# Shorter opening run of maxima, setup steps moved into the main loop, and the two PV steps of a round set apart

## The chip, the cores and the metric
The kernel runs on one core of one Trainium2 chip. Time is device time of one execution in microseconds (us). Before the change the median of three runs is 1162.82 us (1160.92 to 1167.73). The engines are PE (TensorE: matmuls and transposes), DVE (VectorE), ACT (ScalarE), POOL (GpSimd) and SP, which here only issues DMAs. Each runs its own list of instructions strictly in order and waits on semaphores.

## The reference
One transformer block with adaptive layer norm, float32, on x of 4 batches x 1024 tokens x 256 features:

```
mod = silu(c) @ wmod  -> sa, ca, ga, sb, cb, gb   (ga, gb: pushed to at least 0.25 in size)
h = layernorm(x) * (1 + ca) + sa
x = x + ga * (softmax(q k^T / 4) v @ proj_w.T + proj_b)     16 heads of 16
h = layernorm(x) * (1 + cb) + sb
per group of 1024 tokens: of 8 encoders/decoders take the one with the least
  mean((relu(h We + be) Wd + bd - h)^2); its adapter is relu(h Wdown + bd) Wup + bu
x = x + gb * (h W_base + b_base + adapter)
```

## The kernel before
Attention of the four batches is the main loop. It is cut into 256 units: a unit is 4 heads, one half of the queries (512) and 128 keys. For each unit PE does four "E" matmuls (keys x queries, transposed scores, 50 rows: 48 of split operands and two rows that hold minus the row maximum), ACT takes the exponential of each into `P` (L831), and PE does the unit's "PV" step (`PV`, four groups of 17 columns in the single bank `pO`). The row maxima that the two extra rows hold come from "M" matmuls (queries x keys, `pM`), which DVE reduces one by one (L953). 32 M belong to the 8 units of one head group and query half ("hq", 0 to 31). After the 32nd, `mmax` joins them on DVE, POOL splits them in two halves (L1255), PE transposes them (`mturn`, L605), ACT copies them (L846), and SP writes them into the operand `QO` with four DMAs (L1358). M must therefore run ahead of E. E uses three banks (`pE`), M three banks (`pM`), everything else mostly one bank (`pX`).

All engines walk one list of steps, made by `order()` on the host. It has three parts. First the opening: layer norm, q, k and v of batch 0. Then `LEAD` (56) M steps with nothing of E between them; there M takes five banks in turn (`pM` and two of `pE`). Between each five of them stands one item of `beside`: `setupa`, `setupb`, `setupq`, `setupc` (products of decoder weights and biases that later choose the adapter, with DVE work behind each) and two halves of `qk 0,1,0` (the next query projection). Then 128 rounds of the main loop. I call them **pair 0 to pair 127**, since each has two units: 8 E, up to 8 M, two PV. A pair is three bursts of 3, 3 and 2 E/M couples (`BURSTS`). Behind burst 1 stand PV of the two units before. Behind bursts 2 and 3 stand "long" steps (pieces of projection, encoder, gram and so on) in number set by a credit, taken from the table of due units in `plan()`; "short" steps (transposes) stand behind burst 3, "quiet" steps (no PE) in between. A pair that finds no long step due has only E, M and PV for PE. Batch b begins at pair 32b.

A query or key projection (`qk`) leaves PSUM as `hi` (ACT, L881) and `lo` (DVE, L1048), and SP then copies pieces of both into `QO` or `KO` with twelve DMAs (`copy`, L1349). There is one `hi`/`lo` buffer: the next `qk` can write `hi` only when all twelve have landed. The copies stand in SP's list two per burst, and so do `mturn`'s four DMAs, in the order of the list; SP waits at `mturn` until ACT has written `mT`.

Of the kernel before, what the change touches and what calls it, by code (L numbers as in the profile page):

```python
# [11 lines left out]
ALU = mybir.AluOpType  # L12
# [9 lines left out]
NM = 32 * 8 * NB  # L22
# [14 lines left out]

SHARE = 1.45

LEAD = 56  # L40

MB, EB, XB, SB = (0, 1, 2), (3, 4, 5), (6,), (5, 2)

SEQ = [(gi, c) for gi in range(4 * NB - 4) for c in range(2)]
# [4 lines left out]
def plan():  # L51

    due = {}

    def at(u, *steps):
        due.setdefault(u, []).extend(steps)

    at(0, ("gates",))
    at(5, ("qk", 0, 1, 1, 0), ("qk", 0, 1, 1, 1))
    for b in range(NB + 1):  # L60
        B = UB * b
        if b >= 1:
            q = b - 1
            halves = ((B - 31, (0, 1)), (B, (2, 3))) if q == LAST else ((B + 3, (0, 1, 2, 3)),)
            for u, ks in halves:
                for th in sorted({k // 2 for k in ks}):
                    if q == LAST or th == 1:
                        at(u - 1, ("atturn", q, th), ("atturn", q, 2 + th))
                for k in ks:
                    at(u, ("proj", q, k), ("bn2", q, k), ("ln2s", q, k), ("ln2n", q, k), ("xsq", q, k))  # L70
                    at(u, ("xturn", q, k))
                for t in range(2 * ks[0], 2 * ks[-1] + 2):
                    at(u + 1, ("enc", q, t))
                for p in range(4):
                    at(u + 2, ("half", q, p, ks[0] // 2) if q == LAST else ("gram", q, p))
            at(B + 6, ("pick", q), ("select", q), ("fetch", q))
            if q == LAST:
                for k in range(4):
                    at(B + 6 if k > 1 else B - 10, ("base", q, k))
            for h in range(2):  # L80
                at(B + 7, ("mid", q, h), ("out", q, 2 * h), ("out", q, 2 * h + 1))
        if b < NB:
            if b:
                at(B + 0, ("qk", b, 1, 0, 0), ("qk", b, 1, 0, 1))
                at(B + (4 if b == LAST else 6), ("qk", b, 1, 1, 0), ("qk", b, 1, 1, 1))
            if b < LAST:
                at(B + 55, ("atturn", b, 0), ("atturn", b, 2))
            at(B + (36 if b == LAST else 60), ("prep", b))
        if b + 1 < NB:
            for k in range(4):  # L90
                at(B + 11, ("ln1load", b + 1, k), ("ln1s", b + 1, k), ("ln1n", b + 1, k), ("ln1turn", b + 1, k))
            at(B + 33, ("qk", b + 1, 0, 0, 0), ("qk", b + 1, 0, 0, 1))
            at(B + 38, ("qk", b + 1, 0, 1, 0), ("qk", b + 1, 0, 1, 1))
            at(B + 44 if b else B + 18, *(("v", b + 1, k) for k in range(4)))
    return due


def before(s):

    if len(s) == 1:  # L100
        return []
    kind, b, a = s[0], s[1], s[2:]
    if kind == "ln1load":
        return [(("ln1turn", b, a[0] - 1), 0)] if a[0] else []
    if kind == "ln1s":
        return [(("ln1load", b, a[0]), 1)]
    if kind == "ln1n":
        return [(("ln1s", b, a[0]), 1)]
    if kind == "ln1turn":
        return [(("ln1n", b, a[0]), 1)] + ([(("qk", b - 1, 1, 1, 1), 0)] if b else [])  # L110
    if kind == "qk":
        return [(("ln1turn", b, 2 * a[2] + i), 1) for i in range(2)]
    if kind == "v":
        return [(("ln1turn", b, a[0]), 1)]
    if kind == "atturn":

        return [(("oturn", turned(b, a[0])), 1)] + ([(("gram", b - 1, 3), 0)] if b else [])
    if kind == "prep":
        return [(("out", b - 1, 3), 1)] if b else []
    if kind == "proj":  # L120
        return [(("atturn", b, a[0] // 2 + i), 0) for i in (0, 2)] + [(("prep", b), 4)]
    if kind == "bn2":
        return [(("proj", b, a[0]), 0)]
    if kind == "ln2s":
        return [(("bn2", b, a[0]), 0)]
    if kind == "ln2n":
        return [(("ln2s", b, a[0]), 1)]
    if kind == "xsq":
        return [(("ln2n", b, a[0]), 1)]
    if kind == "xturn":  # L130
        return [(("ln2n", b, 2 * (a[0] // 2) + i), 1) for i in range(2)]
    if kind == "enc":
        return [(("xturn", b, 2 * (a[0] // 4) + i), 1) for i in range(2)]
    if kind == "gram":
        return [(("enc", b, t), 1) for t in range(8)]
    if kind == "half":
        return [(("enc", b, 4 * a[1] + t), 1) for t in range(4)]
    if kind == "base":
        return [(("xturn", b, 2 * (a[0] // 2) + i), 1) for i in range(2)]
    if kind == "pick":  # L140
        return [(("half", b, 3, 1) if b == LAST else ("gram", b, 3), 0)] + [(("xsq", b, k), 0) for k in range(4)]
    if kind == "select":
        return [(("pick", b), 1)]
    if kind == "fetch":
        return [(("select", b), 0)]
    if kind == "mid":
        return [(("fetch", b), 2)]
    if kind == "out":
        return [(("mid", b, a[0] // 2), 0)] + ([(("base", b, a[0]), 0)] if b == LAST else [])
    return []  # L150
# [7 lines left out]
def copies(n, w):  # L158


    return [("copy", n, w, g, i) for g in (0, 1) for i in range(12 if (n, w, g) == (0, 0, 0) else 6)]


def order():
# [4 lines left out]
    for w in (1, 0):  # L169
        for half in range(2):  # L170
# [3 lines left out]

    out += [(("v", 0, t), p) for t in range(4) for p in range(2)] + [("modmm", 1), ("modmm", 2)]

    beside = deque([[("setupa",)], [(("qk", 0, 1, 0, 0), p) for p in range(2)], [("setupb",)],
                    [(("qk", 0, 1, 0, 1), p) for p in range(2)], [("setupq",)], [("setupc",)]])
    for i in range(LEAD):
        out.append(("M", i))  # L180
        if i % 5 == 4 and beside:
            out += beside.popleft()
        if i == 31:
            out.append(("mmax", 0))
        if i == 37:
            out.append(("mturn", 0))
    due, m = plan(), LEAD
    moving, waiting, begun = deque(copies(1, 0)), {"short": [], "long": [], "quiet": []}, []
    done = {("ln1turn", 0, k): -9 for k in range(4)}

    def come(u):
# [5 lines left out]
    def next_of(queue, u):  # L197

        if queue == "long" and begun:
            return begun.pop()  # L200
        for s in waiting[queue]:
            if all(done.get(p, u + 1) + lag <= u for p, lag in before(s)):
                waiting[queue].remove(s)
                return (s, 0) if s[0] in PIECES else s
        return None

    def put(s, u):
        out.append(s)
# [33 lines left out]
    for u0 in range(0, NU, 2):  # L242
        if u0 % 8 == 0 and u0:
            waiting["short"].append(("oturn", u0 // 8 - 1))
        come(u0)
        come(u0 + 1)
        tiles = deque((u0 + i // 4, i % 4) for i in range(8))
        for n, pairs in enumerate(BURSTS):
            u = u0 + 2 * n / 3
            if n == 2:  # L250

                short = [s for s in (next_of("short", u) for _ in range(2)) if s]
            for _ in range(pairs):
                out.append(("E", *tiles.popleft()))
                maximum()
            for _ in range(3 if u0 >= UB * LAST else 2):
                if moving:
                    out.append(moving.popleft())
            s = next_of("quiet", u)
            if s:  # L260
                put(s, u)
            if n == 0:
                if u0:
                    out += [("PV", u0 - 2), ("PV", u0 - 1)]
            else:
                if n == 2:
                    for s in short:
                        put(s, u)
                credit = long(u, min(credit + (SHARE if u0 < UB * LAST else 2), 2.5))
            s = next_of("quiet", u)  # L270
            if s:
                put(s, u)
# [84 lines left out]
def adaln_block(nc, x, wqkvT, wpT, pb, wbase, bbase, wenc, benc, bencc, wdec, wdecT, bdecT,  # L357
                wdown, bdown, wup, bup, cidx, cT, wmod, consts, out):
    ctx = ExitStack()
    with ctx:  # L360
# [577 lines left out]
        def vector(e):  # L938
# [4 lines left out]
            for s in S.list:  # L943
# [58 lines left out]
                elif kind == "gates":  # L1002
# [3 lines left out]
                    for k, o in ((0, 512), (1, 1280)):  # L1006
# [8 lines left out]
                                               in1=gt[:, k, 1, :], op0=ALU.add,  # L1015
                                               op1=ALU.mult).then_inc(*(link.up() if k == 0 else (s_gates, 1)))

                elif kind == "ln1s":
                    b, k = s[1:]
                    xt = tokens(b, k)  # L1020
# [151 lines left out]
                                    ALU.add).then_inc(*empties(s))  # L1172

                elif kind == "setupa":
                    e.memset(be[:, :, :], 0.0).then_inc(*link.up())
                    dve.wait_ge(*link.now())
                    dve.wait_ge(d_w[2], 16)
                    dve.wait_ge(d_cst, 16)
                    for p in range(4):
                        a = e.tensor_scalar(be[:, p, 2 * p:2 * p + 2], bmask, bec[:, p:p + 1], None, ALU.mult)  # L1180
                    a.then_inc(s_be, 1)
                    dve.wait_ge(*full(*s))
                    dve.wait_ge(d_w[3], 16)
                    e.tensor_tensor(bT[:, :, :], bank(s)[:, 0:16].rearrange("p (c n) -> p c n", c=2), bdT[:, :, :],
# [262 lines left out]
```

## Time and profile before

| | |
|---|---|
| median of three runs | 1162.82 us |
| the profiled execution | 1166.85 us |
| its span | 1165.0 us |
| PE busy | 1085.9 us (93%), 5820 matmuls |
| DVE busy | 814.1 us (70%) |
| ACT busy | 643.3 us (55%) |
| M reductions, DVE L953 | 630.0 us in 1002 recorded (1024 in the program) |
| mean granted TensorE clock | 0.94 of 2.4 GHz |

The span runs from the first to the last instruction of the profiled execution, which lies 1.85 us under its own time and 4.0 us over the median with it. PE's busy share reads higher than its work: E and M matmuls that follow each other at the pace of DVE are recorded as overlapping. The places of pairs in time are read from the starts of the 1024 E matmuls, all of which are in the trace: pair 0 starts at 85.03 us, pair 7 at 140.28, pair 15 at 200.98, pair 32 at 324.85, pair 112 at 969.86 and pair 127 at 1097.99.

### The profile page before, as it was taken

To read this page: it belongs to the slowest core of one execution; us is meant where nothing else is said; L and a number is where in the kernel's file an instruction comes from. 1 tells how busy PE (TensorE), PEld (TensorE's weight loads), DVE (VectorE), ACT (ScalarE), POOL (GpSimd) and SP (SyncE) were. 2 spreads that over 40 slices of the span, in tenths; PEclk is the share of its full clock that TensorE was granted. 3 is DMA by queue.
4 is the path that set the end of the run, shared out by engine and by line. 5 is a ranking of instruction groups with operands and counts; after the bars stand their busy time and mean duration, and the time that the engine had idled before them with its cause. 6 is when DMAs were issued, how large, how long until landed. Compare 5 with 4: busy or idle time off the path is not lost.

```text
span 1165.0 us, 15950 instructions
## 1 busy us (share of the span) xinstructions
PE 1085.9 (93%) x5820; PEld 512.3 (44%) x5820; DVE 814.1 (70%) x1593; ACT 643.3 (55%) x1293; POOL 126.4 (11%) x251
## 2 busy tenths in 40 slices
PE   6898999989999999999999999999999999989966
PEld 3443344333334345454444344455443455434534
DVE  3486777767878887786778887777688766672133
ACT  3105667656756666665666666665666555556510
POOL 3000121000030121000301120000300000210000
PEclk9757899988999999999999999999899999979989
DMA  7612400240115100330233000411170000200001
GB/s 224 95 19 38 65 20 10 39 58 15 41 40 76 28 19 2 56 60 29 64 55 64 11 20 10 73 34 38 55 100 11 2 2 14 83 1 2 1 1 41
DMA packets 31345, 47.02 MB, mean 40 GB/s; under 512 B 6611, under 2 KB 23512, under 8 KB 31260
## 3 DMA queue, kind: packets, MB, share of 16 engines
q1 hardware_dynamic: 30564, 45.15, 19.6%
q0 software_dynamic: 288, 0.79, 0.4%
q8 instruction: 46, 0.75, 0.3%
q14 instruction: 31, 0.25, 0.1%
q10 hardware_dynamic: 416, 0.07, 0.0%
HBM read 15.95 MB, written 4.22 MB: 17 GB/s over the span
## 4 chain that ended last, share of the span: by engine, by line
PE 72%; DVE 11%; ACT 6%; SPq 3%; DMA 3%; issue 2%; POOL 1%; ACTq 0%; DVEq 0%; POOLq 0%
PE pX L558 21%; PE pO L558 21%; PE pE L558 18%; PE pM L558 10%; DVE mx L953 6%; ACT P L831 4%; DMA QO<-lo 2%; SPq L1349 2%; ACT hi L881 1%; DVE lo L1048 1%; SPq L1347 1%; DMA x<-in_x 1%; SPq L1358 1%; PE pE L635 1%; DVE X L1084 1%
## 5 line engine op out<-in xcount | busy, mean ns | idle before, releaser
L953 DVE TENSOR_REDUCE mx<-pM 128x1 f32<-128x512 f32 x1002 | 630.0, 683 | 178.4 <-PE pM L558 176.5
L831 ACT ACTIVATE P<-pE 128x512 f32<-128x512 f32 x1024 | 544.5, 599 | 334.5 <-PE pE L558 333.1
L558 PE MATMUL pE<-QO,KO 50*128 50x512 f32 x1024 | 373.4, 452 | 18.8 <-ACT P L831 12.8
L558 PE MATMUL pM<-KO,QO 48*128 48x512 f32 x1002 | 373.8, 469 | 12.0 <-DVE mx L953 9.2
L558 PEld LDWEIGHTS pE<-QO,KO 50*128 50x128 f32 x1024 | 170.1, 191 | 273.9 <-issue 194.4
L558 PE MATMUL pO<-P,V 128*17 128x512 f32 x2048 | 268.6, 646 | 0.0
L558 PEld LDWEIGHTS pM<-KO,QO 48*128 48x128 f32 x1002 | 165.5, 193 | 46.8 <-DVE mx L953 35.5
L558 PEld LDWEIGHTS pO<-P,V 128*17 128x17 f32 x2048 | 49.3, 101 | 140.5 <-issue 140.2
L558 PE MATMUL pX<-h1T,wqkv_s 128*128 128x512 f32 x116 | 65.6, 676 | 9.1 <-DVE lo L1048 8.2
L1255 POOL CAST mh<-mxc 128x16 fp32r<-128x16 f32 x32 | 6.5, 204 | 544.6 <-DVE mxc L962 544.6
L558 PE MATMUL pX<-wenc_s,h2T 128*128 128x512 f32 x108 | 55.0, 619 | 1.5 <-DVE Hb L1103 1.2
L558 PE MATMUL pX<-X,Hb 128*128 128x258 f32 x200 | 51.5, 393 | 1.2 <-DVE lo L1048 1.1
L558 PEld LDWEIGHTS pX<-X,Hb 128*128 128x128 f32 x200 | 35.4, 190 | 13.3 <-issue 7.3
L881 ACT ACTIVATE hi<-pX 128x512 fp32r<-128x512 f32 x28 | 16.7, 598 | 42.6 <-PE pX L558 22.8
L838 ACT ACTIVATE osb<-pO 128x512 f32<-128x512 f32 x32 | 19.1, 598 | 37.7 <-PE pO L558 37.7
L1048 DVE SCALAR_TENSOR_TENSOR lo<-pX,hi 128x512 fp32r<-128x512 f32 x28 | 19.4, 691 | 27.4 <-ACT hi L881 27.4
L558 PEld LDWEIGHTS pX<-h1T,wqkv_s 128*128 128x128 f32 x116 | 20.3, 203 | 32.1 <-issue 18.8
L1103 DVE TENSOR_TENSOR Hb<-pX,nbe 128x512 f32<-128x512 f32 x27 | 18.5, 686 | 18.2 <-PE pX L558 18.2
L558 PE MATMUL pX<-Hb 128*128 128x128 f32 x216 | 30.6, 292 | 0.0
L558 PEld LDWEIGHTS pX<-Hb 128*128 128x128 f32 x216 | 28.1, 202 | 5.0 <-issue 4.5
L558 PE MATMUL pX<-wbg,h2T 128*128 128x256 f32 x112 | 29.6, 389 | 0.2 <-ACT mid L936 0.2
L1240 POOL TENSOR_SCALAR xin<-xin,mv,rs 128x256 f32<-128x256 f32 x24 | 29.3, 1227 | 1.1
(211 smaller groups left out, 764.9 us busy)
## 6 DMA issues: line engine op xcount, KB each, us to landing
QO<-hi SPq DMA_DIRECT2D x60, 128.0 KB, 4.4
KO<-hi SPq DMA_DIRECT2D x56, 128.0 KB, 4.1
x<-in_x SPq DMA_DIRECT2D x4, 1024.0 KB, 7.1
out<-x SPq DMA_DIRECT2D x16, 256.0 KB, 2.2
QO<-lo SPq DMA_DIRECT2D x30, 128.0 KB, 4.6
KO<-lo SPq DMA_DIRECT2D x28, 128.0 KB, 4.5
xin<-in_x SPq DMA_DIRECT2D x12, 256.0 KB, 2.7
QO<-mT SPq DMA_DIRECT2D x128, 4.0 KB
```

The source lines that it names most:

```text
L558: return e.matmul(o, lhsT, rhs, start=start, stop=stop)
L635: a = e.transpose(o[:, 256 * c + 128 * t:256 * c + 128 * t + 128], tokens(b, k)[:, t, 128 * c:128 * c + 128], ident)
L831: e.activation(P[:, u % 3, j, :], bank(s), ACT.Exp).then_inc(*empties(s))
L838: e.activation(osb[:, :], pO[:, :], ACT.Copy).then_inc(s_osb, 1)
L881: e.activation(halves(oc, w, b)[0][:, cs], bank(s), ACT.Copy, scale=1.0 if w else 0.25).then_inc(s_hi, 1)
L953: e.tensor_reduce(mx[:, hq % 2, k:k + 1, kh], bank(s), AX.X, ALU.max, negate=True).then_inc(*empties(s))
L1048: e.scalar_tensor_tensor(out=lo_[:, cs], in0=bank(s), scalar=1.0 if w else 0.25, in1=hi_[:, cs].bitcast(F), op0=ALU.mult, op1=ALU.subtract ...
L1084: e.scalar_tensor_tensor(out=X[:, t, 0:D], in0=x2[:, t, :], scalar=mv2[:, t, 0:1], in1=bc[:, 2, :], op0=ALU.subtract, op1=ALU.mult).then_i ...
L1103: e.tensor_tensor(Hb[:, t, :], bank(s), nbe[:, :], ALU.max).then_inc(*empties(s))
L1240: a = e.tensor_scalar(xt[:, t, :], xt[:, t, :], mv1[:, k, t, 0:1], rs1[:, k, 1, t:t + 1], ALU.subtract, ALU.mult)
L1347: e.dma_start(*move(0, 0, 0, i, src, slice(512 * c, 512 * c + 512))).then_inc(d_q0[c], 16)
L1349: e.dma_start(*move(w, slot, g, i, src)).then_inc(landed(n, w, g)[0], 16)
```

## The change
`LEAD` goes from 56 to 48. `beside` is gone: its `qk` halves become due in unit 0, the four setup steps in unit 8 with an order among them (`SETUP`), and `gates` in unit 4. DVE's filling of `be` moves from `setupa` into `gates`. The copies of `qk 0,1,0` now enter SP's list when that step is done. And the second PV of a pair moves from behind burst 1 to behind burst 2 wherever fewer than two long steps are ready and M steps are left; there the credit is cut so that at most one long step follows.

```diff
-LEAD = 56
+LEAD = 48
+SETUP = {"setupb": [(("setupa",), 1)], "setupq": [(("setupb",), 1)], "setupc": [(("setupq",), 0)]}
...
-    at(0, ("gates",))
-    at(5, ("qk", 0, 1, 1, 0), ("qk", 0, 1, 1, 1))
+    at(0, ("qk", 0, 1, 0, 0), ("qk", 0, 1, 0, 1))
+    at(6, ("qk", 0, 1, 1, 0), ("qk", 0, 1, 1, 1))
+    at(4, ("gates",))
+    at(8, ("setupa",), ("setupb",), ("setupq",), ("setupc",))
...
-    beside = deque([[("setupa",)], [(("qk", 0, 1, 0, 0), p) for p in range(2)], [("setupb",)],
-                    [(("qk", 0, 1, 0, 1), p) for p in range(2)], [("setupq",)], [("setupc",)]])
     for i in range(LEAD):
         out.append(("M", i))
-        if i % 5 == 4 and beside:
-            out += beside.popleft()
...
-    moving, waiting, begun = deque(copies(1, 0)), {"short": [], "long": [], "quiet": []}, []
+    moving, waiting, begun = deque(), {"short": [], "long": [], "quiet": []}, []
...
+    def ready(u):
+
+        return len(begun) + sum(all(done.get(p, u + 1) + lag <= u for p, lag in before(s)) for s in waiting["long"])
...
             if n == 0:
                 if u0:
-                    out += [("PV", u0 - 2), ("PV", u0 - 1)]
+                    out.append(("PV", u0 - 2))
+
+                    later = m < NM and ready(u) < 2
+                    if not later:
+                        out.append(("PV", u0 - 1))
             else:
                 if n == 2:
                     for s in short:
                         put(s, u)
+                elif u0 and later:
+                    out.append(("PV", u0 - 1))
+                    credit = min(credit, 1 - SHARE)
                 credit = long(u, min(credit + (SHARE if u0 < UB * LAST else 2), 2.5))
```

PE, behind the first ten M steps or so, before (M is written to pM and pE from KO,QO; `be,wd` and `bT,Hb` are setupa and setupb, `h1T,wqkv_s` is qk 0,1,0):

```order
L558 MATMUL pE<-be,wd 128x8 x8
L558 MATMUL pM<-KO,QO 128x512 x3
L558 MATMUL pE<-KO,QO 128x512 x2
L558 MATMUL pX<-h1T,wqkv_s 128x512 x2
L558 MATMUL pM<-KO,QO 128x512 x3
L558 MATMUL pE<-KO,QO 128x512 x2
L558 MATMUL pE<-bT,Hb 128x8 x8
```

PE at the end of the opening run, after; the last row is the first E of pair 0 (operands QO,KO):

```order
L570 MATMUL pM<-KO,QO 128x512 x3
L617 MATMUL pE<-cst,mhl 32x128
L570 MATMUL pE<-KO,QO 128x512 x2
L570 MATMUL pM<-KO,QO 128x512 x3
L570 MATMUL pE<-KO,QO 128x512 x2
L570 MATMUL pM<-KO,QO 128x512 x3
L570 MATMUL pE<-QO,KO 128x512
```

The opening run now has M alone, apart from the transpose of hq 0's maxima (`mhl`), and ends eight M earlier.

SP from the DMAs of hq 0's maxima (`QO<-mT`) to those of hq 1's, before (`QO<-hi`, `QO<-lo` are the copies of qk 0,1,0, `modd<-X` belongs to gates):

```order
L1358 DMA QO<-mT 2x4x128 x4
L1349 DMA QO<-hi 16x2x1024 x2
L1349 DMA QO<-lo 16x2x1024
L1349 DMA QO<-hi 16x2x1024
L1363 DMA modd<-X 4x1536
L1349 DMA QO<-hi 16x2x1024
L1349 DMA QO<-lo 16x2x1024
L1349 DMA QO<-hi 16x2x1024 x2
L1349 DMA QO<-lo 16x2x1024
L1349 DMA QO<-hi 16x2x1024 x2
L1349 DMA QO<-lo 16x2x1024
L1358 DMA QO<-mT 2x4x128 x4
```

The same copies on SP after:

```order
L1371 DMA QO<-mT 2x4x128 x4
L1362 DMA QO<-hi 16x2x1024 x2
L1362 DMA QO<-lo 16x2x1024
L1362 DMA QO<-hi 16x2x1024
L1376 DMA modd<-X 4x1536
L1362 DMA QO<-hi 16x2x1024
L1362 DMA QO<-lo 16x2x1024
L1371 DMA QO<-mT 2x4x128 x4
L1362 DMA QO<-hi 16x2x1024 x2
L1362 DMA QO<-lo 16x2x1024
L1362 DMA QO<-hi 16x2x1024 x2
L1362 DMA QO<-lo 16x2x1024
```

Six of the twelve copies now stand behind hq 1's maxima. In batch 1 and 2's query copies (pairs 17 to 19, 33 to 35, 65 to 67) four stand behind the maxima, where before ten stood behind them but a pair earlier.

PE in pair 23, which has no long step, after, from its first PV (unit 44) to its second (45); `free` and a number is the bank that is waited for (`order` rows with their waits):

```order
L570 MATMUL pO<-P,V 17x512 x4
L570 MATMUL pE<-QO,KO 128x512 [waits free3]
L570 MATMUL pM<-KO,QO 128x512 [waits free0]
L570 MATMUL pE<-QO,KO 128x512 [waits free4]
L570 MATMUL pM<-KO,QO 128x512 [waits free1]
L570 MATMUL pE<-QO,KO 128x512 [waits free5]
L570 MATMUL pM<-KO,QO 128x512 [waits free2]
L570 MATMUL pO<-P,V 17x512 x4
```

And before, pair 23 from its first burst to both PV:

```order
L558 MATMUL pE<-QO,KO 128x512 [waits free3]
L558 MATMUL pM<-KO,QO 128x512 [waits free0]
L558 MATMUL pE<-QO,KO 128x512 [waits free4]
L558 MATMUL pM<-KO,QO 128x512 [waits free1]
L558 MATMUL pE<-QO,KO 128x512 [waits free5]
L558 MATMUL pM<-KO,QO 128x512 [waits free2]
L558 MATMUL pO<-P,V 17x512 x8
```

One row of eight PV matmuls has become two of four with three E/M couples between them. This holds in 48 of the 128 pairs.

## Rows read from the trace of the kernel before
**Rows 1.** Windows: stretch, its us; busy us of each engine; granted clock, DMA share.
```profile
37.20:85.03 47.83, 40.97 (x118) 22.67 (x118) 37.55 (x78) 2.05 (x4) 0.57 (x3) 0.62 0.32 48
85.03:140.28 55.25, 49.08 (x223) 19.78 (x223) 40.64 (x76) 31.73 (x61) 4.55 (x10) 0.80 0.34 54
140.28:200.98 60.70, 57.35 (x315) 26.25 (x315) 44.69 (x84) 40.55 (x81) 11.30 (x18) 0.94 0.05 15
200.98:324.85 123.87, 114.41 (x588) 44.14 (x589) 89.76 (x153) 78.14 (x151) 7.46 (x18) 0.92 0.21 39
206.80:215.78 8.98, 8.74 (x42) 3.31 (x42) 6.56 (x11) 5.87 (x11) 0.00 (x0) 1.00 0.00 0
228.81:241.46 12.65, 10.37 (x38) 3.20 (x39) 6.75 (x11) 5.38 (x10) 0.00 (x0) 0.81 0.65 84
248.38:257.06 8.68, 7.76 (x34) 2.70 (x33) 6.01 (x13) 4.34 (x9) 0.58 (x3) 0.80 0.82 122
277.42:283.95 6.53, 5.94 (x34) 2.49 (x34) 5.37 (x12) 4.06 (x9) 0.57 (x3) 1.00 0.02 4
350.93:360.57 9.64, 8.56 (x39) 3.09 (x39) 8.28 (x18) 5.79 (x13) 0.94 (x2) 1.00 0.57 71
603.53:613.55 10.02, 8.57 (x40) 3.09 (x39) 8.27 (x18) 5.79 (x13) 0.93 (x2) 1.00 0.62 76
969.86:1097.99 128.13, 122.06 (x637) 58.50 (x636) 65.07 (x139) 71.56 (x144) 13.78 (x26) 0.92 0.07 23
1097.99:1165.04 67.05, 45.91 (x211) 28.25 (x210) 20.05 (x62) 10.48 (x25) 3.31 (x6) 0.90 0.06 18
```
**Rows 2.** Waits of DVE, 37 to 85 us: total, times, longest.
```profile
DVE lo L1048 <- ACT hi L881: 4.7, 2, 3.5
DVE bT L1184 <- PE pE L558: 3.3, 1, 3.3
```
**Rows 3.** Timeline of DVE in the opening run: start, us, instruction.
```profile
39.72 1.28 DVE L953 TENSOR_REDUCE mx<-pE 128x1 f32<-128x512 f32 x2
...
76.52 1.88 DVE L953 TENSOR_REDUCE mx<-pM 128x1 f32<-128x512 f32 x3
...
79.51 1.88 DVE L953 TENSOR_REDUCE mx<-pM 128x1 f32<-128x512 f32 x3
```
**Rows 4.** Timeline of PE: setupa and setupc in the opening run.
```profile
41.79 3.17 PE L558 MATMUL pE<-be,wd 128*128 128x8 f32 x16 [3.08 <-issue]
...
65.72 3.78 PE L558 MATMUL pX<-Hb 128*128 128x128 f32 x16
```
**Rows 5.** Timeline of DVE in pair 25, with its idle time before.
```profile
281.87 3.08 DVE L953 TENSOR_REDUCE mx<-pM 128x1 f32<-128x512 f32 x5 [1.10 <-PE pM L558]
```
**Rows 6.** Waits of DVE, 140 to 229 us.
```profile
DVE mx L953 <- PE pM L558: 20.4, 15, 2.5
```
**Rows 7.** Waits of DVE, 241 to 325 us.
```profile
DVE mx L953 <- PE pM L558: 21.9, 15, 2.9
```
**Rows 8.** Pairs 19, 35: SP's timeline, the chain of waits, ACT's timeline.
```profile
223.75 2.62 SPq L1358 DMA_DIRECT2D QO<-mT  x4
...
232.12 6.23 DMA QO<-lo
...
238.43 0.60 ACT L881 ACTIVATE hi<-pX 128x512 fp32r<-128x512 f32 x1 [2.35 <-DMA QO<-lo]
...
358.14 0.60 ACT L881 ACTIVATE hi<-pX 128x512 fp32r<-128x512 f32 x1 [0.82 <-PE pX L558]
```
**Rows 9.** Timeline of PE behind the last E.
```profile
1107.49 0.63 PE L669 MATMUL pM<-cst,Atok 128*128 128x128 f32 x4 [0.97 <-DVE Atok L978]
1108.89 1.97 PE L558 MATMUL pX<-wpg,h1T 128*128 128x256 f32 x8 [0.78 <-ACT h1T L903]
...
1133.01 1.98 PE L558 MATMUL pE<-X,Hb 128*128 128x258 f32 x8 [0.88 <-DVE Hb L1103]
...
1135.71 1.91 PE L558 MATMUL pE<-X,Hb 128*128 128x258 f32 x8
```

More of the change, by code:

```diff
@@ L100, in before @@
     if len(s) == 1:
-        return []
+        return SETUP.get(s[0], [])
     kind, b, a = s[0], s[1], s[2:]
@@ L1016, in vector @@
                                                op1=ALU.mult).then_inc(*(link.up() if k == 0 else (s_gates, 1)))
+                    e.memset(be[:, :, :], 0.0).then_inc(*link.up())
+                    dve.wait_ge(*link.now())
+                    dve.wait_ge(d_w[2], 16)
+                    dve.wait_ge(d_cst, 16)
+                    for p in range(4):
+                        a = e.tensor_scalar(be[:, p, 2 * p:2 * p + 2], bmask, bec[:, p:p + 1], None, ALU.mult)
+                    a.then_inc(s_be, 1)
                 elif kind == "ln1s":
@@ L1174, in vector @@
                 elif kind == "setupa":
[L1175 to L1181, printed above, removed]
                     dve.wait_ge(*full(*s))
```

## The prediction, made before the changed kernel was timed
> **What bounds the kernel now.** I read the page first: PE is busy 93% of the span and DVE 70%, so most of the loop is PE's, but that share hides who sets the pace. Then the table of windows, cut at the starts of pairs. Where pairs carry long steps, PE has real work throughout: pair 16, with three qk pieces, takes 8.98 us with PE busy 8.74 [rows 1]. Pairs with none take far more than their PE work: pair 25 takes 6.53 us at full clock. Its eight reductions come every 0.60 us (five in 3.08), and before them DVE stood idle for 1.10 us, waiting for PE [rows 1, 5]. So such a pair is 8 x 0.60 = 4.8 us of reductions, some 0.3 of other DVE work, and a hole in which PE did 16 PV matmuls in a row while the three M banks ran empty. The holes add up to 20.4 us in pairs 7 to 18 and 21.9 us in pairs 20 to 31 [rows 6, 7].
>
> The opening run, 37.20 to 85.03 us, is DVE's as well: five reductions start in 79.51 - 76.52 = 2.99 us, 0.598 each [rows 3], while the clock is mostly at its lower level, 1.2 GHz (mean 0.62) [rows 1]. DVE also waits there for steps that stand between M: 4.7 us for `hi`, 3.3 for setupa [rows 2]. The end, from pair 112, is a chain of dependent steps beside the last E [rows 1].
>
> **The opening run.** M 0 to 4 are reduced by 39.72 + 1.28 = 41.0 us [rows 3]. With nothing between, DVE goes straight on. Pair 0's first E takes the bank that M 43 leaves: 39 further reductions x 0.598 = 23.3 us and one mmax, so 64.5 us, where it started at 85.03. Could something else hold it? It needs hq 0's maxima in `QO`. M 31 is reduced at 41.0 + 27 x 0.598 = 57.1; the way from there through POOL, PE, ACT and four DMAs I estimate at 6 us (2.62 for the four issues [rows 8], the rest small instructions and a landing): 63, just in time. **-20** (-18 to -21).
>
> **Pairs 0 to 6** hold 55.25 us [rows 1]. Added: four qk pieces at (8.98 - 6.53) / 3 = 0.8 us each [rows 1], 3.3 us. The setup steps: setupa and setupc took 3.17 and 3.78 us at 1.2 GHz [rows 4], so half at 2.4; with setupb about 5 us on PE, and 3 us on DVE beside it. Bounds: 0, if all falls into holes of pairs 4 to 6, and 9 at the lower clock; I take 4. Gained: qk fills PE in pairs 0 and 1, so I expect the clock back earlier than now, where the stretch has a mean of 0.80 [rows 1]: -4.
>
> Then the wait that the change adds. `hi` of qk 0,1,1 (pair 3) is free when twelve copies have landed. Six of them now stand on SP behind the four DMAs of hq 1's maxima, and SP waits at those until ACT has run at the end of pair 2. Queued behind is everything of SP; who waits is ACT at `hi`, with its exponentials behind it, hence PE's E banks. From the start T of pair 3: ACT and the first issue 0.8 us, the four DMAs 2.62, five issues of 0.63 to the last, and 6.23 from that issue to landing [rows 8]: T + 12.8. Pair 19 is the measured example: its last copy landed at 232.12 + 6.23 = 238.35, that is T + 9.5, ACT waited 2.35 us, and the pair took 12.65 [rows 1, 8], 3.1 more than the landing. So pair 3 should take 15.9 where some 8.5 were enough: +7. Bounds: 0, if copies overlap better than in pair 19, and +9 with the lower clock behind it. `gates` on DVE gets `be` with it: 0.7 us more in pair 2, covered by three filled M banks only in part; +0.3. Sum: 3.3 + 4 - 4 + 7.3 = 10.6; since four of these pairs also get the split PV I take **+8** (-3 to +14).
>
> **Pairs 7 to 14** hold 60.70 us [rows 1], all eight with PV split. Between two bursts PE is now away for one PV instead of two, so of the 1.10 us hole [rows 5] I expect some 0.2 to remain: -0.9 at full clock, up to twice that at half clock. With v pieces the second half of the gain is PE's own, since five couples no longer follow each other at DVE's pace. The 20.4 us of holes [rows 6] lie over 12 pairs, 1.7 each; I take 1.0 of it: **-8** (-12 to 0).
>
> **Pairs 15 to 31** hold 123.87 us [rows 1]; all but pairs 16 and 19 split. 21.9 us of holes in twelve pairs are 1.8 each [rows 7]; 15 pairs x 0.95 = 14. Against it pair 19: four copies stand behind hq 5's maxima, which come a pair later, so the last lands at T + 0.8 + 2.62 + 3 x 0.63 + 6.23 = T + 11.5 instead of 9.5: +2. **-12** (-20 to +2).
>
> **Pairs 32 to 111** are PE's; pieces move between pairs, their sum stays. Pair 35 had no such wait (0.82 us, for PE [rows 8]) and took 9.64 us; with landing at T + 11.5 and 3 us behind it, 14.2. Pair 67 took 10.02 [rows 1] and goes the same way. That is +4.4 each. In pair 98 the maxima move behind all copies, -1.5, and the four near-empty pairs at the ends of batches 1 and 2 give -2. **+5** (0 to +12).
>
> **The end.** Split pairs may place one long step only, so out 2 ends a pair later, prep 3 and proj 3 with it; xturn 3 moves from pair 120 to 122 and 123, and eight `half` and four `base` pieces that stood in pairs 124 to 126 now stand in and behind pair 127. From 969.86 to 1097.99 are 128.13 us [rows 1]. Without the twelve pieces (three half pieces take 1135.71 - 1133.01 = 2.7 us [rows 9], so 11 us) they take at most 117. I take 116. Behind 1097.99, the waits of 0.97 and 0.78 us [rows 9] take in about 2 of the 11 us: 67.05 + 9 = 76. **-3** (-12 to +8).
>
> Also moved and priced at nothing: each hq's maxima come one pair later relative to their E. From transpose to last landing I estimate 5 to 6 us (2.62 of it the issues [rows 8]); a pair is left for it. If pairs drop under 5.5 us, E waits by the difference, eight hq's of a few tenths.
>
> **Sum.** -20 + 8 - 8 - 12 + 5 - 3 = -30 us, on the profiled execution's 1166.85 us: 1137. That execution lies 4.0 us over the median of the runs, so I predict 1162.8 - 30.5 = 1132 us. Differences under 0.5%, 6 us, can't be told from no change.
>
> **Rivals.**
> 1. The split gives nothing: the exponentials or bank turns take the place of the hole. For it: ACT's eight exponentials are 4.06 us of pair 25's 6.53 [rows 1], and they stall at each PV too. Against: they leave 2.4 us. Then -8 and -14 go: the sum is -8.5: 1154.
> 2. The deferred pieces are not absorbed: the end costs +12 instead of -3, because xturn 3 stands in pairs that are short of PE work and the rest of the chain starts later. For it: 67.05 us behind pair 127 with PE busy for 45.91 [rows 1]. Against: twelve pieces leave pairs that had been full. 1132 + 15 = 1147.
> 3. More comes out: copies land as in pair 19 at worst (7 + 2 + 9 us not lost) and holes close fully. 1132 - 18 = 1114.
> 4. Slower: the clock. The split spreads PE's work thin, and the opening run shows the clock at 0.62 where M alone runs at DVE's pace [rows 1]. Pair 21, without a long step and at a mean of 0.80, took 8.68 us [rows 1] against 6.8 for the 15 pairs on average ((123.87 - 8.98 - 12.65) / 15). If the 22 or so pairs without long steps all went that way, +1.9 x 22 = +42 would stand in place of -22. With the other terms, -8, that is +34: 1197. It decides from 8 / 22 = 0.36 us more per pair than today. Against it: today's runs of couples without a PV between are longer than any that are left, and the stretch 200.98 to 324.85 still holds a mean of 0.92 [rows 1].
>
> The Trainium skill (TensorE: Matmul & The Clock Gate, A second HAM failure mode: psum-queue depth-cycling) says that a PE which idles briefly and often between groups of matmuls, as it goes round PSUM banks, swings between its two clocks. This speaks for rival 4, since the change doubles the switches between E/M and PV; the trace has such swings in these pairs, but with PE's pauses as long as they are before the split.
>
> **Chances.** The forecast 52%, with its own range 1121 to 1143; rival 3 15%; rival 1 14%; rival 2 12%; rival 4 7%. Faster: all of the forecast and of 3, nearly all of 2 and two thirds of 1 (it ends 9 us below, with 6 the bound): 0.88. Within: the rest of 1 and 2, 0.06. Slower: 0.06. From 1115 to 1156 I leave out rival 4, half of rival 3 and the edge of 1: 2 in 10.
>
> **What would show it.** The first E matmul at 64 to 66 us. Eight reductions in a row every 0.6 us with no hole over 0.3 in pairs 20 to 31, and that stretch (241.46 to 324.85 now, 6.9 us a pair) at 5.5 to 6.2 us a pair. ACT waiting for DMA at `hi` in pairs 3, 19, 35 and 67, by 4 to 7 us in pair 3. The stretch behind pair 127 at 75 to 77 us. A first E after 68 us, low clock in most split pairs, or E waiting for `mT`'s DMAs would make the forecast wrong.

## The result, and the profile after
The changed kernel takes 1153.02 us (median of nine runs, 1148.24 to 1158.81), the kernel before 1162.82 us in the same comparison. The ratio is 0.990 (95% interval 0.987 to 0.993): 9.8 us faster, where 30.5 were forecast. A second comparison gave 1153.0 us against 1165.4, ratio 0.9895 (0.988 to 0.991).

The profiled execution took 1148.24 us. It is the fastest of its nine, 4.8 us below their median, while that of before lay 4.0 above its own. So the two profiles differ by 18.6 us, and 8.8 of that is the choice of executions. The totals say little:

```profile
span 1146.4 us, 15955 instructions
PE 1064.5 (93%) x5820; PEld 494.6 (43%) x5820; DVE 814.1 (71%) x1593; ACT 644.1 (56%) x1293; POOL 127.0 (11%) x251
PEclk8668899899999999999999999999999999988989
```

The windows, cut at the starts of pairs, do (columns as in [rows 1]: the stretch, its us, busy us of PE, PEld, DVE, ACT and POOL, granted clock, DMA share, GB/s). In order: the opening run, pairs 0 to 6, 7 to 14, 15 to 31, 35, 67, 112 to 126, and what is behind the start of pair 127.

```profile
37.20:62.87 25.67, 25.09 (x45) 11.55 (x44) 25.64 (x45) 0.27 (x1) 0.57 (x3) 0.54 0.41 63
62.87:131.64 68.77, 60.24 (x283) 25.58 (x282) 46.84 (x99) 33.30 (x63) 4.54 (x10) 0.77 0.32 51
131.64:185.44 53.80, 52.82 (x315) 22.70 (x314) 45.19 (x84) 39.93 (x79) 11.30 (x18) 0.97 0.06 16
185.44:294.94 109.50, 100.41 (x590) 37.25 (x589) 90.14 (x153) 77.82 (x152) 11.04 (x23) 0.95 0.24 45
...
318.75:330.08 11.33, 8.80 (x40) 3.13 (x39) 8.88 (x20) 5.80 (x14) 0.94 (x2) 0.98 0.29 49
574.58:585.74 11.16, 8.63 (x39) 3.13 (x38) 8.70 (x20) 5.79 (x14) 0.94 (x2) 0.99 0.29 50
944.33:1070.12 125.79, 113.16 (x598) 47.98 (x597) 67.44 (x139) 71.01 (x143) 14.02 (x26) 0.92 0.08 23
...
1070.12:1146.44 76.32, 57.37 (x271) 37.93 (x270) 22.92 (x76) 10.58 (x25) 3.31 (x6) 0.90 0.05 16
```

Against [rows 1]: the first E came at 62.87 us instead of 85.03. Pairs 7 to 31 took 163.3 us instead of 184.6, and their clock rose. Pairs 0 to 6 took 68.8 instead of 55.3. Pairs 112 to 126 took 125.8 where 116 were forecast, and 76.3 us follow, as forecast.

The holes of DVE have shrunk. These are its waits for PE in pairs 7 to 18 and 20 to 31 (131.64 to 211.72 and 224.30 to 294.94 us; total, times, longest), and the five reductions of pair 25 with the idle time before them; they answer to [rows 5 to 7].

```profile
DVE mx L965 <- PE pM L570: 10.1, 15, 1.6
```
```profile
DVE mx L965 <- PE pM L570: 7.7, 14, 1.7
```
```profile
259.38 3.16 DVE L965 TENSOR_REDUCE mx<-pM 128x1 f32<-128x512 f32 x5 [0.24 <-PE pM L570]
```

20.4 us have become 10.1, and 21.9 have become 7.7; the 1.10 us hole of pair 25 is 0.24.

The first of the two large waits of the changed kernel stands in pair 3 (87.14 to 104.67). SP's timeline, the chain of waits with the last copy's way to memory, and ACT's timeline; they answer to [rows 8].

```profile
90.65 2.62 SPq L1371 DMA_DIRECT2D QO<-mT  x4
93.31 1.23 SPq L1362 DMA_DIRECT2D QO<-hi  x2
...
96.48 0.59 SPq L1362 DMA_DIRECT2D QO<-lo  x1
```
```profile
96.48 4.73 DMA QO<-lo
```
```profile
101.29 0.60 ACT L893 ACTIVATE hi<-pX 128x512 fp32r<-128x512 f32 x1 [4.27 <-DMA QO<-lo]
```

Six copies follow `mT`'s four issues, and ACT sits 4.27 us before `hi`, with the exponentials behind it.

The second is in pair 118 (993.41 to 1006.03 us). POOL's timeline, and PE's with the transpose of hq 30's maxima:

```profile
996.22 1.30 POOL L1285 TENSOR_TENSOR wpg<-wp_s,bc 128x512 f32<-128x512 f32 x1 [35.55 <-DMA bc<-modd]
...
999.52 5.49 POOL L1296 TENSOR_TENSOR x<-x,bc 128x256 f32<-128x256 f32 x8
1004.94 0.20 POOL L1268 CAST mh<-mxc 128x16 fp32r<-128x16 f32 x1
...
1005.36 0.22 POOL L1274 TENSOR_TENSOR mhl<-mxc,mh 128x16 f32<-128x16 f32 x1
```
```profile
1005.73 0.37 PE L617 MATMUL pE<-cst,mhl 128*32 128x128 f32 x1 [7.37 <-POOL mhl L1274]
```

`prep 3` (8.8 us on POOL, from 996.22 to 1005.01) stands ahead of the splitting of the maxima, so PE idles for 7.37 us at `mturn 30`. It already stood there before the change, where PE came later and waited 1.93 us. These are the same rows of the kernel before:

```profile
1016.80 5.53 POOL L1283 TENSOR_TENSOR x<-x,bc 128x256 f32<-128x256 f32 x8 [0.70 <-DMA x<-in_x]
1022.27 0.20 POOL L1255 CAST mh<-mxc 128x16 fp32r<-128x16 f32 x1
```
```profile
1023.06 0.37 PE L605 MATMUL pE<-cst,mhl 128*32 128x128 f32 x1 [1.93 <-POOL mhl L1261]
```

From about the start of the wait of the changed kernel to the end of pair 119 the mean clock is 0.70, and pair 119 takes 9.3 us:

```profile
998.02:1015.36 17.34, 9.97 (x45) 3.73 (x41) 6.39 (x11) 5.59 (x11) 7.50 (x13) 0.70 0.01 3
```

Pairs 117 to 119 together took 26.87 us before and 27.25 now. Their mean clock is 0.81 in both. These are the rows of pairs 117 to 119 before, and of pairs 121 to 126 before and now:

```profile
1013.21:1040.08 26.87, 24.07 (x118) 10.72 (x117) 18.11 (x38) 13.28 (x27) 10.74 (x18) 0.81 0.08 26
1051.53:1097.99 46.46, 46.38 (x249) 23.01 (x250) 8.00 (x27) 27.52 (x55) 0.58 (x3) 1.00 0.00 1
```
```profile
1023.43:1070.12 46.69, 42.90 (x202) 15.96 (x201) 14.39 (x34) 28.79 (x62) 1.83 (x5) 0.93 0.00 1
```

By the lists of steps, pairs 121 to 126 held 24 pieces of long steps before and hold 12 now, with the last eight M in pair 121. They take as long as before.

### The profile page after: what moved, and what is told of

Same layout as the page of the kernel before. It is cut to its first block, busy times and chain, and to the rows that moved or that the text cites. A ratio compares the mean times of both kernels' runs of the same rounds, so it can differ in the third digit from the quotient of the medians.

```text
span 1146.4 us, 15955 instructions
## 1 busy us (share of the span) xinstructions
PE 1064.5 (93%) x5820; PEld 494.6 (43%) x5820; DVE 814.1 (71%) x1593; ACT 644.1 (56%) x1293; POOL 127.0 (11%) x251
## 4 chain that ended last, share of the span: by engine, by line
PE 77%; DVE 10%; ACT 4%; DMA 3%; SPq 3%; issue 2%; POOL 1%; ACTq 0%; DVEq 0%
PE pX L570 23%; PE pE L570 20%; PE pO L570 20%; PE pM L570 10%; DVE mx L965 5%; DMA QO<-lo 2%; ACT P L843 2%; SPq L1362 1%; DVE lo L1068 1%; ACT hi L893 1%; SPq L1371 1%; DVE X L1104 1%; PE pE L681 0%; PE pE L617 0%; POOL x L1296 0%
## 5 line engine op out<-in xcount | busy, mean ns | idle before, releaser
L570 PE MATMUL pE<-QO,KO 50*128 50x512 f32 x1024 | 367.4, 449 | 15.1 <-ACT P L843 7.3
L570 PEld LDWEIGHTS pO<-P,V 128*17 128x17 f32 x2048 | 43.0, 98 | 116.1 <-issue 116.1
L570 PE MATMUL pX<-X,Hb 128*128 128x258 f32 x208 | 54.5, 395 | 2.4 <-DVE lo L1068 1.5
L1123 DVE TENSOR_TENSOR Hb<-pX,nbe 128x512 f32<-128x512 f32 x26 | 17.9, 687 | 29.7 <-PE pX L570 29.7
L570 PE MATMUL pX<-wqkv_s,h1T 128*128 128x256 f32 x104 | 27.1, 391 | 0.9 <-DVE accA L1132 0.9
```

The costliest lines, as they stand in the source:

```text
L570: return e.matmul(o, lhsT, rhs, start=start, stop=stop)
L1123: e.tensor_tensor(Hb[:, t, :], bank(s), nbe[:, :], ALU.max).then_inc(*empties(s))
```

## The experiments
Each ran in five rounds beside the kernel before, whose median was 1165.4 us in the first four, 1164.0 in the next four and 1164.7 in the last four. "The change" stands for its second measurement, 1153.0 us. Theory A is the forecast's mechanism plus two waits that eat it: copies behind maxima on SP, and maxima behind `prep` on POOL. The rivals are told in each expectation. Stretches are read from one execution, which does not always lie at its kernel's median: the profiled ones of experiments 2 and 9 are 4.9 and 6.4 us under it, those of 3, 4, 6, 11 and 12 are 4.9, 3.2, 6.7, 3.2 and 3.7 us over it, and the others lie within 1.4 us.

**1. The change once more.**

> The changed kernel once more, unedited, for a second profile. The first one was of its fastest execution (1148.2 us against a median of 1153.0), the one of before lay 4 us over its median. Theory A (the two profiles tell the terms right, and what differs between executions of one kernel is the clock in a few pairs): pair 0 again at 62.9 us within 1 us, pair 3 at 16 to 18 us, pairs 20 to 31 within 3 us of the first profile, and the span differs by the granted clock in single pairs, 2 to 8 us in all. Rival B (the gain of the split pairs was luck of that one execution): pairs 20 to 31 take 5 us or more longer than in the first profile.

1153.0 us (1150.5 to 1155.4). Its profile is close to its median (1153.53 us). Two stretches, pairs 121 to 126 and what is behind the start of pair 127, show what one execution of this kernel has and another has not:

```profile
1022.05:1073.92 51.87, 48.69 (x203) 18.03 (x202) 14.37 (x34) 29.13 (x62) 1.83 (x5) 0.77 0.00 1
1073.92:1151.73 77.81, 58.94 (x271) 38.13 (x270) 22.92 (x75) 10.59 (x25) 3.31 (x6) 0.87 0.05 16
```

Pairs 121 to 126 at a mean clock of 0.77 are 51.87 x 0.23 / 0.5 = 24 us at 1.2 GHz. The first profile had 6.8 us of it there, and 46.7 us in all. Everything ahead of pair 118 repeats within 0.5 us.

**2. The split alone.** Before, with the split of PV and its cap; `ready` is the same as in the change. POOL's `fetch` also waits for its own earlier split of maxima, which stands ahead of it in POOL's own list.

```diff
-                    out += [("PV", u0 - 2), ("PV", u0 - 1)]
+                    out.append(("PV", u0 - 2))
+                    later = m < NM and ready(u) < 2
+                    if not later:
+                        out.append(("PV", u0 - 1))
...
+                elif u0 and later:
+                    out.append(("PV", u0 - 1))
+                    credit = min(credit, 1 - SHARE)
```

> The kernel before with the PV split and its limit on long steps alone; opening, LEAD 56 and copies as before. (A wait of POOL for its own last instruction is added before the fetch step.) Theory A (opening -22, first pairs +13, split -21 in pairs 7 to 31, copies behind the maxima +4 to +7, end +7, the end by the split's limit): pair 0 stays at 85 us, no wait for the copies in pairs 3 and 35, pairs 7 to 31 shorter by 15 to 20 us, the stretch from pair 112 on 3 to 8 us longer than before: 1145 to 1152 us. Rival B (the end's loss is of the eight M steps that come later, not of the split): the end is as before, 1140 to 1145. Rival C (the split gives little without the new opening): 1158 or more.

1147.6 us, ratio 0.984 (0.982 to 0.987): better than the whole change. Pairs 20 to 31 take 69.5 us instead of 83.4, pairs 0 to 6 52.7 instead of 55.3, and the stretch behind pair 127 takes 76.0: that 9 us is the split's, by its cap. But pairs 112 to 120 take 74.0 us instead of 81.7 and pairs 121 to 126 44.7 instead of 46.5, so from pair 112 to the end it is 194.7 us against 195.2 before, not the 3 to 8 us more that were expected.

**3. All but the split.**

```diff
-                    later = m < NM and ready(u) < 2
+                    later = False
```

> The changed kernel with the PV split taken out (both PV behind burst 1 everywhere); LEAD 48, moved setup steps and copies stay. Theory A: pair 0 at 63 us, pair 3 about 17 us, pair 7 at about 133 us (7 us earlier than before), pairs 7 to 31 as before, pairs 35 and 67 longer by 1.5 to 3 us each, the end within 3 us of before: 1155 to 1161 us. Rival B: the end 7 us longer than before also here, so 1163 or more.

1159.8 us, ratio 0.996 (0.994 to 0.998). The first E comes at 63.0 us, and most of these 22 us is lost again: pairs 0 to 6 take 70.1 us instead of 55.3, pairs 32 to 111 649.6 instead of 645.0, and pairs 20 to 31

```profile
232.63:319.50 86.87, 82.86 (x411) 32.15 (x410) 61.14 (x105) 54.11 (x105) 10.43 (x20) 0.85 0.19 38
```

against 70.64 with the split and 83.4 before. Behind pair 127 stand 66.9 us. The two parts alone give 17.8 + 5.6 = 23.4 us, together 12.4, which is 11 short. In the profiles this loss stands at the end: from pair 112 on, each part alone takes 194.7 and 193.7 us (before: 195.2), both together 206.9 (experiment 1).

**4. The change with LEAD 56** (and the wait at `fetch` as in 2). Everything else of the change is kept.

```diff
-LEAD = 48
+LEAD = 56
```

> The changed kernel with LEAD 56 again; setup steps stay in the main loop, split stays. (A wait of POOL for its own last instruction is added before the fetch step.) Theory A (most of the opening's gain is the steps taken from between M, not the eight M; hq's maxima come a pair earlier again and the copies stand before them less): pair 0 at 67.7 us (eight reductions of 0.6 later), pair 3 shorter than 17.5 us since the six copies no longer stand behind the maxima of hq 1, about 12 us, pairs 35 and 67 1 to 3 us shorter: 1146 to 1152 us, a few us under the changed kernel. Rival B (the eight M count in full, nothing comes back): 1157 us or more.

1141.9 us, ratio 0.978 (0.976 to 0.980): 11 us faster than with 48, although the first E comes 7.3 us later. The maxima now stand elsewhere against copies and `prep`: pairs 35 and 36 take 17.1 us (21.7), 67 to 69 24.9 (29.7), pair 3 14.6 (17.5), and 117 to 119 21.0 (25.4 to 27.3); in pairs 117 to 119 PE has no wait for POOL. The time lies under the range expected, 1146 to 1152. This turned "48 instead of 56" into the question.

**5. Copies ahead of the maxima, LEAD 48.**

```diff
                     for s in short:
+                        if s[0] == "mturn":
+                            while moving:
+                                out.append(moving.popleft())
                         put(s, u)
```

> The changed kernel (LEAD 48) with one edit: whatever of the twelve copies is still pending goes on SP ahead of mturn's four DMAs. Theory A (in pairs 3, 19, 35 and 67 ACT waits at hi for copies that stand behind a waiting mturn): pair 3 takes 12 to 15 us instead of 17.5, pairs 35 and 36 17 to 18 instead of 21.7, pairs 67 to 69 25 to 26.5 instead of 29.7; sum 8 to 12 us less, ratio to the changed kernel about 0.991. Rival (the copies land late because sixteen DMAs share the queues, whatever their order on SP, and then E waits for the maxima instead): these stretches keep their length, within 2 us in all.

1145.9 us, ratio 0.984 (0.981 to 0.987), 7 less than the change. Pairs 3, 35 and 67:

```profile
87.88:102.51 14.63, 10.42 (x38) 3.46 (x39) 9.25 (x22) 5.53 (x11) 0.00 (x0) 0.77 0.53 76
315.46:326.41 10.95, 10.00 (x41) 3.48 (x40) 8.64 (x20) 5.90 (x14) 0.94 (x2) 0.84 0.37 45
570.39:580.38 9.99, 8.56 (x39) 3.12 (x38) 8.64 (x19) 5.80 (x14) 0.94 (x2) 1.00 0.34 44
```

Pair 3 fell by 2.9 us, 35 and 36 together by 1.7 (less than expected), 67 to 69 by 2.7. The order on SP is the cause, but only for 7.3 of the 12.4 us by which LEAD 56 shortens these pairs. In pair 3 ACT still waits 1.50 us for a DMA at `hi`, and the pair takes 14.6 us as it does with LEAD 56. In pair 35 ACT no longer waits for a DMA there; what is left is not shown, and the clock has a mean of 0.84.

**6. `mmax 30` ahead of `prep 3`, LEAD 48.** One exchange in the list, nothing else moves.

```diff
-            if all(done.get(p, u + 1) + lag <= u for p, lag in before(s)):
+            if all(done.get(p, u + 1) + lag <= u for p, lag in before(s)) and (s != ("prep", LAST) or m >= 992):
...
-[(("prep", b), 4)]
+[(("prep", b), 3 if b == LAST else 4)]
```

> The changed kernel with one exchange: prep 3 stands behind mmax 30 in the list instead of ahead of it (its 8.8 us on POOL no longer come before the splitting of hq 30's maxima); proj 3,0 keeps its place. Theory A (pair 118 is long because PE waits 7.4 us at mturn 30 for POOL behind prep 3): pair 118 takes 5.5 to 6.5 us instead of 12.6, proj 3,0 may wait up to 2 us longer for wpg; together with less low clock behind it, 4 to 9 us less. Rival (PE would wait there anyway, for DVE's reductions or in pair 119 for proj): pairs 117 to 121 take the same in sum, within 1.5 us.

1142.3 us (1139.4 to 1149.0), ratio 0.981 (0.978 to 0.984). POOL's timeline, then PE's:

```profile
1000.24 0.22 POOL L1274 TENSOR_TENSOR mhl<-mxc,mh 128x16 f32<-128x16 f32 x1
1001.73 1.30 POOL L1285 TENSOR_TENSOR wpg<-wp_s,bc 128x512 f32<-128x512 f32 x1 [1.27 <-DMA bc<-modd]
```
```profile
1003.80 0.28 PE L617 MATMUL pE<-cst,mhl 128*32 128x128 f32 x1
...
1010.71 1.51 PE L570 MATMUL pX<-wpg,h1T 128*128 128x256 f32 x4 [2.05 <-POOL x L1296]
```

The 7.37 us wait is gone; 2.05 of it come back at `proj 3`. Pair 118 takes 5.4 us instead of 12.6, pairs 117 to 119 21.4 instead of 25.4 (experiment 1) to 27.3 (the first profile). The medians differ by 10.7, more than these 4 to 6, and more than the 4 to 9 expected. Its profile is its slowest run, so the rest can't be placed; less low clock in pairs 121 to 126 (6.8 us in this profile, 24 in experiment 1) may be part of it, which isn't shown.

**7. No split in batch 3, LEAD 48.**

```diff
-                    later = m < NM and ready(u) < 2
+                    later = m < NM and ready(u) < 2 and u0 < UB * LAST
```

> The changed kernel without the split (and so without its cap on long steps) in batch 3, pairs 96 to 127. Theory A (the cap defers half and base to behind pair 127): the stretch behind pair 127 takes 67 us instead of 76 to 78, pair 118 has no wait for POOL; against it pairs 97 to 115 lose their filled holes, about +5. Pairs 96 to 127 and what is behind together: 3 to 8 us less than the changed kernel. Rival (the end is a chain of dependent steps whose length the cap does not set): sum unchanged or longer.

1141.7 us, ratio 0.982 (0.979 to 0.985), 11.3 less than the change, more than expected. Pairs 121 to 126, and what is behind pair 127:

```profile
1025.64:1072.52 46.88, 46.88 (x258) 23.52 (x257) 13.10 (x35) 26.93 (x54) 0.57 (x3) 1.00 0.00 1
1072.52:1139.67 67.15, 45.69 (x211) 28.26 (x210) 20.02 (x62) 10.47 (x25) 3.31 (x6) 0.92 0.06 18
```

258 matmuls in pairs 121 to 126 instead of 202 and a full clock, in the same 46.9 us. The twelve pieces that the cap pushed behind pair 127 are back in there and cost nothing.

**8. LEAD 56, no cap in batch 3** (and the wait at `fetch` as in 2).

```diff
-                    credit = min(credit, 1 - SHARE)
+                    if u0 < UB * LAST:
+                        credit = min(credit, 1 - SHARE)
```

> LEAD 56 and the split everywhere, without the cap in batch 3. Against the LEAD 56 kernel with the cap (1141.9 us): theory A: the stretch behind pair 127 goes from 76 to 67 us, and the pieces cost about 3 to 5 in pairs 114 to 126: 3 to 7 us less, 1135 to 1139. Rival (the split behind two long steps is worth nothing without the cap, or a new wait stands in pairs 120 to 126 for the steps that come earlier): 1142 or more.

1140.8 us, ratio 0.980 (0.978 to 0.983), which can't be told apart from 4 (1141.9 us, 0.978): a miss. The stretch behind pair 127 is 68.4 us instead of 77.6, but with `out` and `prep` earlier, pairs 112 to 120 take 81.4 us instead of 73.3: `prep 3` stands close before hq 30's maxima again, and PE waits 3.4 us for POOL at `mturn 30`. Pairs 121 to 126 took 46.0 us.

**9. The setup steps later, LEAD 48.**

```diff
-    at(8, ("setupa",), ("setupb",), ("setupq",), ("setupc",))
+    at(20, ("setupa",), ("setupb",), ("setupq",), ("setupc",))
```

> The changed kernel with the four setup steps due in unit 20 instead of 8: they stand in pairs 11, 13 and 15 instead of 4, 5 and 6. Theory A (the forecast's +4 for them, beyond what holes take): pairs 4 to 6 take 22 to 24 us instead of 27.0, pairs 7 to 18 at most 1 more than 80.1; whole 3 us less. Rival 1 (the missing 5 us of pairs 0 to 6 are the setup steps'): pairs 4 to 6 fall by 7 or more. Rival 2 (they are low clock that comes with the pause in pair 3): pairs 4 to 6 fall by less than 2, and low clock stays there.

1159.5 us, ratio 0.996 (0.993 to 0.998): 6.5 slower than the change. Pairs 4 to 6, and 7 to 14:

```profile
103.61:125.59 21.98, 20.80 (x105) 7.22 (x104) 16.56 (x33) 13.53 (x26) 3.98 (x7) 0.84 0.56 84
125.59:186.25 60.66, 60.01 (x347) 28.07 (x348) 46.94 (x96) 40.88 (x81) 11.33 (x18) 0.89 0.05 15
```

Pairs 4 to 6 give 5.0 us (27.0 before), about the forecast's 4. But pairs 7 to 14, which now hold `setupa` and `setupb`, take 6.9 more, at a clock of 0.89 instead of 0.97, so theory A's "at most 1 more" fell. Why the clock stays lower there isn't settled. The profile took 1153.1 us, its kernel's fastest run, so the 6.5 us between the medians aren't placed either.

**10. LEAD 48, edits 5 and 7 together.**

> LEAD 48 with both repairs: pending copies ahead of mturn, and no split in batch 3. If the repairs add up: 1153 - 7 - 11 = 1135 us, 1132 to 1138, with the copies' stretches (pairs 3, 35 and 36, 67 to 69) as in the kernel that had only that edit, and 67 us behind pair 127. If they share a cause: 1140 or more.

1132.4 us (1131.9 to 1135.2), ratio 0.974 (0.970 to 0.977). The two edits add up (1153.0 - 7.2 - 11.3 = 1134.5), so they cure separate losses.

**11. LEAD 48, edits 5 and 8 together.**

> LEAD 48, pending copies ahead of mturn, the split everywhere but without its cap in batch 3. Against the kernel without the split in batch 3: if the split in pairs 97 to 127 pays once the cap is gone, 2 to 5 us less; if not, within 2 us or slower. The stretch behind pair 127 takes 67 to 69 us in both.

1130.3 us (1126.3 to 1137.1), ratio 0.971 (0.967 to 0.975), the lowest median of all; 10 and 11 can't be told apart. Pairs 20 to 31, 112 to 126, and behind pair 127:

```profile
223.25:291.25 68.00, 64.52 (x411) 24.69 (x410) 62.41 (x107) 53.91 (x105) 10.49 (x20) 1.00 0.24 48
944.11:1063.00 118.89, 113.88 (x641) 55.05 (x640) 68.28 (x134) 71.59 (x143) 12.41 (x24) 1.00 0.07 23
1063.00:1131.70 68.70, 47.54 (x211) 29.42 (x210) 20.03 (x62) 10.47 (x25) 3.31 (x6) 0.88 0.06 18
```

**12. The same with LEAD 52.**

> The same with LEAD 52. Theory A: the first E comes 3.5 us later than with 48, and nothing else that LEAD sets is left to lose once the copies and the end are repaired: 3 to 4 us slower than LEAD 48. Rival (pairs 0 to 6 lose by an earlier start what they gain, low clock and waits for hq 1): the same within 1.5 us or faster.

1135.6 us, ratio 0.975 (0.972 to 0.979), 5 more than with LEAD 48; the intervals of 11 and 12 overlap, so that LEAD 48 is the better is likely, not shown. Nor is the later first E (67.2 us, 4.3 later) the cause that the profiles show. Up to pair 112 the two kernels lie 1.0 us apart, and the whole difference stands in pairs 112 to 126, 125.7 us against 118.9. There PE waits for POOL at `mturn 30` again (between 980 and 1025 us; total, times, longest), where `prep 3` stands in pair 116; in experiment 11 it stands in pair 115, and there is no such wait:

```profile
PE pE L621 <- POOL mhl L1278: 5.1, 1, 5.1
```


## Why the prediction was wrong in size
The sum of its terms against the profile of experiment 1, which lies at its kernel's median (pairs cut as in the forecast; this profile is 13.3 us shorter than that of before):

| stretch | forecast | measured |
|---|---|---|
| opening run | -20 | -21.8 |
| pairs 0 to 6 | +8 | +13.5 |
| pairs 7 to 14 | -8 | -6.9 |
| pairs 15 to 31 | -12 | -14.3 |
| pairs 32 to 111 | +5 | +4.5 |
| the end | -3 | +11.8 |
| sum (before rounding) | -30 | -13.3 |

**Right.** The opening run: M at 0.6 us each set the first E (62.87 us, a little ahead of the 64 to 66 forecast). The split: the hole before five reductions fell from 1.10 to 0.24 us, pairs 22 to 31 take 5.4 to 5.7 us, and experiments 2 and 3 give the gain to it alone. The copies behind maxima in pairs 3, 19, 35 and 67: ACT waited 4.27, 3.85, 1.91 and 1.92 us for a DMA at `hi`; pair 3 took 17.5 us (15.9 forecast), pairs 35 and 36 together 3.0 more than before, 67 to 69 3.5 more (4.4 each forecast). But the order on SP is only a part of these times: with the copies first, pair 3 still takes 14.6 us, where the forecast held 8.5 to be enough, and the order is worth 2.9 us of its +7, and 1.7 and 2.7 of the two +4.4 (experiment 5). That pair 3 came out near is partly luck. The stretch behind pair 127 grew by 9.3 to 10.8 us (+9).

**The step that failed** is in the end: "Without the twelve pieces [...] they take at most 117. I take 116." They took 125.8 and 129.1. The forecast took the PE time of the twelve pieces, 11 us, off the length of the pairs that lose them. Pairs 121 to 126 took 46.5 us before with 24 pieces, and with 12 they took 46.7 us in the first profile and 51.9 in experiment 1. With the twelve back, these pairs take 46.9 us without the split and 47.2 with it, at full clock (experiments 7 and 11). In experiment 2, with the old opening, eleven pieces fewer saved 1.8 us. In the first profile pairs 121 and 122, now without a piece, are only 0.8 and 1.1 us shorter (pair 121 also has the last eight M; in experiment 2, without them, it takes 5.4 instead of 7.9 us). Pairs 123 and 124 are 0.3 and 1.9 us longer, with 3.4 us each at 1.2 GHz, and in experiment 1 the six pairs have 24 us at that level, against none before. So this one term is 11 to 16 us off, and the end as a whole 14.8, most of the 17 between forecast and this profile.

**What the forecast did not follow** is `prep 3` on POOL. I had written that out 2 ends a pair later and "prep 3 and proj 3 with it". On POOL hq 30's maxima stand behind `prep 3` before and after, but PE now comes to them earlier against it and waits 7.4 us instead of 1.9. This does not explain the distance to the forecast, since pairs 112 to 120 took 79.1 and 77.3 us against 81.7 before, less than the forecast gave them. It hides a gain that the forecast had not counted: without the wait the same nine pairs take 73.2 us (experiment 6) and 74.0 (experiment 2).

**Mis-sized:** pairs 0 to 6, by 5.5 us. Pair 3 has 1.6 of it, the setup steps 1.0 (5.0 by experiment 9, where 4 were taken). The remaining 3 I put down to the clock: I had counted -4 for an earlier return to 2.4 GHz, but the mean is 0.77 over 68.8 us, 31 us at the lower level, against 0.80 and 22 before [rows 1]. That the pause in pair 3 itself brings low clock is only argued: experiment 5 shortened it and pairs 5 and 6 then ran at low clock longer (pairs 4 to 6 took 28.0 us instead of 27.0).

**The base.** I subtracted from the profile and shifted by the 4.0 us offset, which holds; the sum gives 1132.8, and the forecast takes off 30.5 where its terms give 30. Where the result stands against 1162.8 or 1165.4 is another 2.6 us that no term explains.

**The rivals.** Rival 2 had the place and the size at the end (+12, measured +11.8 in experiment 1 and +6.9 in the first profile), and its main point holds, that the deferred pieces are not absorbed. Whether xturn 3 in short pairs and the later chain are the reasons was not tested. Its price for the whole, 1147, is still 6 us under the result; pairs 0 to 6 alone took 5.5 more than forecast. Rivals 1 and 4 are refuted: the split alone gives 17.8 us (experiment 2), and in pairs 20 to 31 the mean clock rose to 0.96, while without the split it was 0.85 (experiment 3). The Trainium skill's rule (TensorE: Matmul & The Clock Gate, A second HAM failure mode: psum-queue depth-cycling) spoke for rival 4. What depresses the clock by it is short, frequent idling of PE; the split doubles the switches but fills the idling. So the rule itself isn't contradicted, my use of it was: 16 us at low clock in this stretch before became 6.3 after and none in experiment 11.

## What to carry to other kernels
Work that is deferred from a stretch is a saving only if that stretch was bound by it. Look at how long a comparable stretch without the work takes, and not at the busy time of the work: here twelve pieces of 11 us left six pairs, the pairs stayed as long, and the pieces cost 9 us where they went. PE's busy time, 46.4 of 46.5 us before, gave no sign of that. When a step moves, follow it on every engine that runs a part of it, and ask which short, urgent instruction stands behind its long ones: 8.8 us of POOL work ahead of a 0.6 us split held PE for 7.4 us, and the exchange of the two was worth 10.7 us by the medians (4 to 6 of it seen in the profiles). And a constant like LEAD sets how one periodic step (the maxima) meets others (copies, `prep`). 56 beat 48 by 11 us, and after two repairs 48 was ahead of 52 by 5, and both times such meetings were part of the difference. No run compares the values with all of them harmless, so what the earlier first E is worth by itself stays open.

## What the runs showed of the hardware
Pairs 121 to 126 with about half of their 24 pieces (profiles of the change, and of experiments 1, 2, 4, 5, 6 and 9) had 7 to 24 us at 1.2 GHz, differing between executions of the same instructions (6.8 and 24 us); the seven profiles where these pairs keep all pieces (before, and experiments 3, 7, 8, 10, 11 and 12) had none. Pieces of PE work that seem to cost time can thus be free twice: they fill the gap, and the clock stays up. One profile of such a kernel may be 5 to 7 us from its median (4.8 in the first profile here, 6.7 in experiment 6).
